# Half-size blocks for the rest of the routed rows, and a new order of the attention steps, in a decoder layer with eight experts

## The reference

```python
x = x + linear_attention(LN(x))          # q, k = elu(.) + 1; q (k^T v) / (q . sum k + eps), per batch
x = x + softmax(q k^T / 16) v            # q from LN(x), k and v from the context, with biases
xf = LN(x)                               # 4096 rows
shared = gelu(xf @ Wfc_s + bfc_s) @ Wproj_s + bproj_s        # 256 -> 1024 -> 256
gate = softmax over the two largest of xf @ Wr               # 8 experts, 2 per row
routed = sum_e gate[:, e] * (gelu(xf @ Wfc[e] + bfc[e]) @ Wproj[e] + bproj[e])
x = x + shared + routed
```

## Time and profile before

| | |
|---|---|
| median of 3 runs | 862.61 us (862.16 to 863.2) |
| profiled execution, whole time | 864.7 us |
| its span | 863.0 us |
| PE / DVE / ACT / POOL busy | 92% / 73% / 41% / 28% |
| attention steps | from the start to about 266 us |
| shared blocks, routed blocks | about 266 to 441 us, 441 to 852 us |

### The profile page before, as it was taken

The page is one execution under the profiler, slowest core; times in us unless marked ns, Lnnn a source line. Parts: engine busy times, 40 slices in busy tenths (PEclk is TensorE's granted clock), DMA queues, the critical chain, the costliest instruction groups (busy, mean ns, idle before and its releaser), DMA issues.

```text
span 863.0 us, 21653 instructions
## 1 busy us (share of the span) xinstructions
PE 797.6 (92%) x6791; PEld 671.2 (78%) x6791; DVE 632.9 (73%) x2006; ACT 356.8 (41%) x777; POOL 240.6 (28%) x221
## 2 busy tenths in 40 slices
PE   3889898899856999999999999999999999999994
PEld 1666676666644888888888888888888888888884
DVE  4578888988756998888876666666666666666663
ACT  4445454454323555555543333333333333333331
POOL 2210101101110025555503333333333333333333
PEclk9999999999956999999999999999999999999998
DMA  5465676765333567887743434355344434444430
GB/s 178 141 159 137 180 150 170 168 155 119 81 62 84 156 180 239 235 237 238 234 120 62 65 55 69 58 57 70 54 64 63 66 64 63 63 62 64 65 50 7
DMA packets 168045, 98.07 MB, mean 114 GB/s; under 512 B 110316, under 2 KB 163336, under 8 KB 167944
## 3 DMA queue, kind: packets, MB, share of 16 engines
q1 hardware_dynamic: 153640, 79.65, 38.3%
q0 software_dynamic: 14304, 17.10, 11.5%
HBM read 37.84 MB, written 37.88 MB: 88 GB/s over the span
## 4 chain that ended last, share of the span: by engine, by line
PE 67%; issue 22%; DVE 5%; DMA 2%; SPq 1%; ACT 1%; POOL 1%; POOLq 0%; DVEq 0%; ACTq 0%
PE bank_kv L1177 11%; PE bank_st L1163 11%; PE bank_kv L1179 11%; PE bank_st L1165 11%; PE bank_kv L1178 11%; PE bank_st L1164 11%; DMA stage_w<-in_L_ffn_Wfc_s 1%; POOL rstd L519 1%; DVE w_parts L961 1%; DVE w_parts L740 1%; PE bank_st L1097 1%; DVE expert_buffers L973 1%; DMA expert_buffers<-rows_by_expert 0%; SPq L345 0%; PE bank L1116 0%
## 5 line engine op out<-in xcount | busy, mean ns | idle before, releaser
L697 ACT ACTIVATE expert_buffers<-bank_st,bias_columns 128x256 f32<-128x256 f32 x440 | 207.0, 473 | 334.2 <-DVE expert_buffers L974 214.5
L1177 PE MATMUL bank_kv<-w_parts,expert_buffers 128*128 (+1 forms) x880 | 240.6, 273 | 1.0 <-DVE expert_buffers L974 1.0
L1178 PE MATMUL bank_kv<-w_parts,expert_buffers 128*128 (+1 forms) x880 | 240.4, 273 | 0.0
L1179 PE MATMUL bank_kv<-w_parts,expert_buffers 128*128 (+1 forms) x880 | 240.4, 273 | 0.0
L973 DVE TENSOR_SCALAR expert_buffers<-expert_buffers 128x256 f16<-128x256 f32 x440 | 130.2, 296 | 120.4 <-ACT expert_buffers L697 100.2
L974 DVE SCALAR_TENSOR_TENSOR expert_buffers<-expert_buffers 128x256 f16<-128x256 f32 x440 | 188.6, 429 | 15.1
L1163 PE MATMUL bank_st<-expert_buffers,w_parts 128*128 128x256 f16 x624 | 170.1, 273 | 1.3 <-DMA expert_buffers<-rows_by_expert 1.3
L1165 PE MATMUL bank_st<-expert_buffers,w_parts 128*128 128x256 f16 x624 | 170.1, 273 | 0.0
L1164 PE MATMUL bank_st<-expert_buffers,w_parts 128*128 128x256 f16 x624 | 170.1, 273 | 0.0
L563 POOL DMA_INDIRECT out<-expert_buffers,token x78 | 121.8, 1561 | 20.6 <-issue 20.2
L1177 PEld LDWEIGHTS bank_kv<-w_parts,expert_buffers 128*128 128x128 f16 x880 | 86.2, 98 | 15.1 <-DVE expert_buffers L974 2.9
(11 more groups left out here) (150 smaller groups left out, 1027.0 us busy)
## 6 DMA issues: line engine op xcount, KB each, us to landing
rows_by_expert<-w_parts SPq DMA_DIRECT2D x13, 795.0 KB, 5.5
stage_w<-in_L_ffn_Wfc SPq DMA_DIRECT2D x16, 512.0 KB
stage_w<-in_L_ffn_Wproj SPq DMA_DIRECT2D x16, 512.0 KB
expert_buffers<-in_L_ffn_bproj SPq DMA_DIRECT2D x39, 128.0 KB
rows<-in_x SPq DMA_DIRECT2D x16, 256.0 KB, 3.2
x_residual<-rows SPq DMA_DIRECT2D x16, 256.0 KB, 4.7
expert_buffers<-x_residual SPq DMA_DIRECT2D x16, 256.0 KB
out<-expert_buffers SPq DMA_DIRECT2D x16, 256.0 KB
```

Of the source, the lines that this page charges most:

```text
L697: act.activation(g32[f % 2], hid[f % 2][:, 0:BLK], ACT.Gelu_apprx_tanh, bias=bias, scale=UNSCALE).then_inc(s["gelu_done"], 1)
L1177: pe.matmul(y, g[:, 0, tile(t)], w_hi, start=f == 0 and t == 0, stop=False, skip_group_check=True)
L1178: pe.matmul(y, g[:, 0, tile(t)], w_lo, start=False, stop=False, skip_group_check=True)
L1179: op = pe.matmul(y, g[:, 1, tile(t)], w_hi, start=False, stop=f == FC - 1, skip_group_check=True)
```

## The change

Routed rows: each expert's rows fill blocks of 256 only as far as these get full, and the rest goes to blocks of 128. The kernel now has 25 full (`FULL`) and 21 half (`HALF`) routed blocks. In the half ones `up` moves 128 columns, ACT writes two chunks into one 256-column buffer, DVE splits them as a pair, `down` makes high-high and high-low in one matmul of 512 columns and low-high in one of 256, six chunks behind `up`, and the two halves of the result are added in `evacuate`. A half block has one scatter. The hidden layer has four PSUM banks for two. `route` has 20 parts in blocks 0 to 4 for 16 in 0 to 3; the scatters start at block 5 and are spread over 10 blocks (before: 4 and 11).

Attention steps: the first norm is applied by ACT (`norm_first`, from a small `shift` of DVE); the context products are made of three fp16 passes (DVE makes the low part of `ctxT`, and once those of `fold`, `wv` and the row vector); the largest two logits are found by `top_two`, for 15 batches in step 19 and for the last in step 20, with comparisons and reductions. The order on each engine is new. TensorE: state, scores, transposed context, attention, transposed probabilities, K and V, Q, probabilities times V, context products, logits. On SP the transposes of the first norm come after the store of x2. ACT converts the first weights behind the first norm's high part.

```diff
-    NRT = 2 * T // BLK + E - 1
+    FULL = (2 * T - E * (BLK - 1) + BLK - 1) // BLK
+    HALF = 2 * T // P + E - 1 - FULL * TB
...
-    SEND_FROM, SEND_BLOCKS = 4, 11
...
+    SEND_FROM, SEND_BLOCKS = 5, 10
...
+    def tiles_in(n):
+
+        return TB if n < FULL else 1
+
...
-        hid = [bank_st[:, c, :] for c in range(2)]
+        hid = [bank_st[:, 0, :], bank_st[:, 1, :], bank3[:, :], bank7[:, :]]
...
+        FIRST_HALF = NSH + FULL
+        LAG_FULL, LAG_HALF = 2, 6
...
-                if live(i + 1):
-                    turn_norm(0, i + 1)
...
                     sp.wait_ge(s["x2_stored"], b * 16)
                     sp.dma_start(tiles_of(x2_dram, b), rows[:, ds(b * TB, TB), 0:D])\
                         .then_inc(s["x2_stored"], 16)
+                if live(i + 1):
+                    turn_norm(0, i + 1)
+                b = i + 3
+                if 1 <= b < B:
+                    sp.wait_ge(s["x_loaded"], b * 16)
+                    sp.dma_start(rows[:, ds(b * TB, TB), 0:D], tiles_of(x_rows, b)).then_inc(s["x_loaded"], 16)
...
+            def load_xT(n):
+
+                if n >= 2:
                     sp.wait_ge(s["up_done"], FC * (n + (NSH - 1)))
-                sp.dma_start_transpose(xT[parity].rearrange("p l k n -> p (l k) n"),
-                                       rows16_dram[ds(n, 1)].rearrange("a r w -> (a r) w")).then_inc(s[f"xT_loaded{parity}"], 16)
+                dst = xT[n % 2] if n < FULL else xT_half[n % 2]
...
+            def norm_first(b):
+
+                act.wait_ge(s["shift_ready"], b)
+                got(act, "lo1_ready", b - 1)
+                for t in range(TB):
+                    op = act.activation(xn[0][:, t, :], rows[:, b * TB + t, 0:D], ACT.Identity,
+                                        bias=shift[:, t:t + 1], scale=rstd[:, t:t + 1])
+                op.then_inc(s["xn1_ready"], 1)
...
+                    got(act, "ctxT_done", i - 2)
+                    copy(ctxT16[:, :, 0, :], ctxT_ps, "ctxT_hi")
...
+                if live(i + 1) and i != -1:
+                    norm_first(i + 1)
+                if live(i - 3):
+                    got(act, "pT_done", i - 3)
+                    got_if(act, "pv_done", i - 4)
+                    copy(probT[0:CK, :], pT_ps[0:CK, :], "pT_copied")
+                if live(i + 1) and i != -1:
+                    high(0, i + 1)
...
+                    if G >= FIRST_HALF:
+                        pair = (c - FC * FIRST_HALF) // 2
+                        spare = g32[pair % 2]
+                        at = slice(f % 2 * P, f % 2 * P + P)
+                        if f % 2 == 0:
+                            act.wait_ge(s["g_ready"], FC * FIRST_HALF + pair - 1 if pair < 2 else c - 2)
...
+            def top_two(batches):
...
+                for j, out_hot in enumerate((best, second)):
+                    count_top(dve.tensor_tensor(part, values, of(j), ALU.is_equal))
+                    count_top(dve.tensor_tensor(part, part, below, ALU.mult))
+                    count_top(dve.tensor_reduce(at, part, AX.X, ALU.min))
+                    count_top(dve.tensor_tensor(out_hot, below, at_e, ALU.is_equal))
+                    if j == 0:
+                        count_top(dve.scalar_tensor_tensor(values, best, -3.0e38, values, ALU.mult, ALU.add))
+                        count_top(dve.tensor_reduce(top[:, 1, ts], values, AX.X, ALU.max))
...
+                sums_of = [(n, b) for n, b in ((0, i + 2), (1, i - 1), (2, i - 3)) if live(b)]
+                if live(i + 2) and i > 0:
+                    sums(i, 0, i + 2, len(sums_of) == 1)
...
+                    dve.scalar_tensor_tensor(shift[:, :], mv[:, 0, :, 0], -1.0, rstd[:, 0:TB], ALU.mult, ALU.mult)\
+                        .then_inc(s["shift_ready"], 1)
...
-                if live(i - 5):
-                    b = i - 5
-                    apart(dve)
-                    got(dve, "logits_copied", b)
-                    for t in range(TB):
-                        op = dve.max(max8[:, t, :], lg[:, t, :])
-                    chain(op, "max_step", b + 1, own=True)
-                    for t in range(TB):
-                        op = dve.max_index(max8_at[:, t, :], max8[:, t, :], lg[:, t, :])
-                    chain(op, "top_step", b + 1)
-                    dve.tensor_copy(top[:, ds(b * TB, TB), :], max8[:, :, 0:2])
-                    dve.tensor_copy(top_f[:, ds(b * TB, TB), :], max8_at[:, :, 0:2]).then_inc(s["top_ready"], 1)
...
+                if i in TOP_STEPS:
+                    top_two(TOP_STEPS[i])
...
+                    dve.tensor_tensor(ctxT16[:, :, 1, :], ctxT_ps, ctxT16[:, :, 0, :], ALU.subtract)\
+                        .then_inc(s["ctxT_lo"], 1)
...
+                elif part == 14:
+                    then(dve.tensor_tensor(beyond, place, over_t(full_rows), ALU.is_ge))
+                elif part == 15:
+                    then(dve.tensor_tensor(beyond, beyond, over_t(jump), ALU.mult))
+                    then(dve.tensor_tensor(place, place, beyond, ALU.add))
...
+                if G >= FIRST_HALF:
+                    y = ybuf[parity][:, 0, :]
+                    chain(dve.scalar_tensor_tensor(y, ysum[parity][:, 0, :], UNSCALE, b2blk, ALU.mult, ALU.add),
+                          "y_part", G - FIRST_HALF + 1)
+                    dve.scalar_tensor_tensor(y, ysum[parity][:, 1, :], UNSCALE, y, ALU.mult, ALU.add)\
+                        .then_inc(s["y_read"], 1)
+                    dve.wait_ge(s["y_read"], G + 1)
+                    dve.tensor_scalar(y, y, gate[parity][:, 0:1], None, ALU.mult).then_inc(s["y_ready"], 1)
...
+                    elif f % 2 == 1:
+                        pair = (c - FC * FIRST_HALF) // 2
+                        got(dve, "gelu_done", c)
+                        dve.wait_ge(s["down_done"], FC * FIRST_HALF + pair - 3 if pair < 4 else c - 7)
+                        g = gs[pair % 4]
+                        dve.tensor_scalar(g[:, 0, :], g32[pair % 2], A_SCALE, None, ALU.mult).then_inc(s["g_hi"], 2)
+                        dve.wait_ge(s["g_hi"], c + 1)
+                        dve.scalar_tensor_tensor(g[:, 1, :], g32[pair % 2], A_SCALE, g[:, 0, :], ALU.mult, ALU.subtract)\
+                            .then_inc(s["g_ready"], 2)
...
-                    got(pe, "ctxT_copied", b)
+                    got(pe, "ctxT_lo", b)
                     for m in range(DK):
                         for k in range(DK):
-                            pe.matmul(k2T_ps[:, m, :], fold[:, k, tile(m)], ctxT[:, k, :], start=k == 0, stop=k == DK - 1)
+                            for a, c in PASSES:
+                                pe.matmul(k2T_ps[:, m, :], fold16[:, k, a, tile(m)], ctxT16[:, k, c, :],
+                                          start=(k, a, c) == (0, 0, 0), stop=(k, a, c) == (DK - 1, 1, 0))
                     for k in range(DK):
-                        pe.matmul(row_ps[0:1, :], row_cols[:, k:k + 1], ctxT[:, k, :], start=k == 0, stop=k == DK - 1)
+                        for a, c in PASSES:
+                            pe.matmul(row_ps[0:1, :], row16_cols[:, k, a:a + 1], ctxT16[:, k, c, :],
+                                      start=(k, a, c) == (0, 0, 0), stop=(k, a, c) == (DK - 1, 1, 0))
                     for k in range(DK):
-                        op = pe.matmul(v2_ps[0:CK, :], ctxT[:, k, :], wv[:, k, :], start=k == 0, stop=k == DK - 1)
+                        for a, c in PASSES:
+                            op = pe.matmul(v2_ps[0:CK, :], ctxT16[:, k, a, :], wv16[:, k, c, :],
...
+                if G >= FIRST_HALF:
+                    g = gs[(c - FC * FIRST_HALF) // 2 % 4][:, :, f % 2 * P:f % 2 * P + P]
+                    y = bank_kv[:, parity, :].rearrange("p (l n) -> p l n", l=2)
+                    both = w2[:, ds(e * 4096 + ((f // 4) * 2048), 2048)].rearrange("p (l n) -> p l n", l=2)
+                    both = both[:, :, (f % 4) * 256:(f % 4) * 256 + D]
+                    pe.matmul(y, g[:, 0, :], both, start=f == 0, stop=False, skip_group_check=True)
+                    pe.matmul(y[:, 0, :], g[:, 1, :], both[:, 0, :], start=False, stop=f == FC - 1, skip_group_check=True)\
+                        .then_inc(s["down_done"], 1)
+                    return
...
                     if f == 2 and isinstance(G, int) and G == NSH:
                         pe.wait_ge(s["w2_lo"], HALVES)
                     up(G, parity, e, f)
-                    if f >= 2:
-                        down(G, parity, e, f - 2)
-                    elif before is not None:
-                        down(G - 1, 1 - parity, e_before, FC - 2 + f)
+                    d = FC * G + f - lag
+                    if d >= 0 and not (G == FIRST_HALF and f < LAG_HALF - LAG_FULL):
+                        down_lagging(d)
```

522 lines of the change are left out of this document (292 added, 230 removed).

## The result

The changed kernel takes 851.71 us (median of 7 runs, 848.70 to 856.37). The kernel before, run on the same chip, takes 862.61 us (7 runs, 859.75 to 865.96). The ratio is 0.9882, 95% interval 0.9847 to 0.9917. The change makes the kernel faster by 10.9 us, 1.2%: the interval excludes no change, but the gain stays under the 2% from which a version is called faster here. The forecast was 809, 54 us faster, in a range of 796 to 829: it was wrong. The profiled execution has a span of 853.1 us, against 863.0 before.

What follows compares the result with a forecast made beforehand. The prediction took TensorE to bound the expert blocks and DVE the attention steps, TensorE close behind. Its terms, the largest -29.1 and -16.6, summed to -54.2 us on a span of 863.0, giving 809 us, range 796 to 829.

Steps and rivals of the forecast that it cites:

- The new order, followed: Attention step: engine order traced through one step; every part is ready before it is wanted, step 11.9 us.
- the wait with least cover: Attention step on SP: the first norm's transpose, now behind the x2 store; landing at 6.4, wanted at 6.8 us.
- work terms (-16.6): Attention steps 4 to 13: less DVE and TensorE work cuts 13.56 to 11.9 us each, -16.6 us in all.
- Rival (C): Attention steps stay at 13.1 us because the first norm's transpose comes late behind the store: 824 us, chance 0.17.
- Half blocks: Routed blocks: 14 full blocks' worth goes, 21 half blocks of 5.6 us come; -29.1 us, from -22 to -35.
- Rival (B): Half blocks: 128-column matmuls go at 81 ns for 56, 25 us more in all: 834 us, chance 0.10.
- the chain through SP: Half blocks: meta copies, row load and transpose stall TensorE, 0.1 us a block, plus 0.2 for scatter packets.
- none binds by itself: Half blocks: ACT, DVE (4.9 us) and POOL (3.9 us) each keep up with TensorE's 5.3 us.
- Rival (D): Half blocks take 6.2 us through the meta, rows, transpose chain or scatter landing, 13 us more: 822 us, chance 0.12.
- the drain: Steps 16 to 20: DVE's max work goes, dearer context part and `top_two` overrun; -3.0 us, from +1 to -6.
- (E): Half blocks: stalls take TensorE's clock down, at 0.50 a block is 10.6 us, 105 more: 914 us, chance 0.03.
- The shared blocks: Shared blocks 1 to 4: 17 more DVE instructions for route parts cost +2.5 us, from 0 to +4.2.

Runs made afterwards that it cites:

- experiment 1: Changed kernel with SyncE issuing the load of batch i+3's x first in its attention step: 832.36 us, ratio 0.9592.
- experiment 2: Changed kernel with VectorE's sums of x moved behind those of x1, late in its step, SyncE's order as changed: 829.57 us, ratio 0.9576.
- experiment 3: Changed kernel with SyncE's x load directly ahead of the x2 store: 824.74 us in a single run.
- experiment 9: Two variants of experiment 7, single runs: no expert number read in half blocks, 806.54 us; fixed expert-0 addresses in full blocks too, 808.18 us.
- experiment 10: Experiment 6 with the 20 route parts three to a shared block over blocks 0 to 6: 821.39 us, ratio 0.9515.
- experiment 7: Experiment 6 with half blocks taking expert 0's weights from fixed addresses, without register steps; a measurement only: 804.84 us, ratio 0.9348.
- experiment 4: Changed kernel with four buffers for the half blocks' transposed rows, so transposes may start one block earlier: 849.09 us, ratio 0.9815.
- experiment 5: Changed kernel with TensorE reading the next block's expert number inside the running block: 858.99 us, ratio 0.9919.
- experiment 6: Changed kernel with SyncE's x load first in its step and four buffers for the half blocks' transposed rows: 821.62 us, ratio 0.9546.
- experiment 8: Experiment 6 with TensorE reading the next block's expert number inside the running block: 819.80 us, ratio 0.9528.

## Why the prediction was wrong

**Attention steps: the step that failed.** "The new order, followed ... All fit, with little room", and "SP's old order had the store last; now the first norm's transpose stands behind it ... the wait with least cover". I followed the store and the transposes but not SP's x load, which the same edit put behind both. And I had `sums(i, 0, i + 2)` only within DVE's total work, where its new place, first in DVE's step, puts the softmax, and through the probabilities K and V, behind a transfer. The runs show it at both ends (experiments 1 to 3). With the wait gone the ten steps are 11.70 us: the forecast of 11.9 was nearly right, and so was the sum of TensorE's work, which had 11.55. So the work terms (-16.6) were right for a kernel that had the x load in time. Rival (C) had the wrong transfer and only part of the loss: 13.1 us a step, where the seven steps at full clock took 13.72 and all ten 14.75 in the mean. That they are longer than before (13.56) is due to the three steps in which the clock fell; a fall of the clock in the attention steps stands in no term and no rival.

**Half blocks: a term too small.** The pace of 56 ns at 128 columns is confirmed: the up matmuls start 0.05 to 0.06 us apart, and eight column blocks of 0.66 us, with 48 of them and the down part, make 5.28 us (forecast 5.3). Rival (B) falls: no run shows its 81 ns, which it puts midway between 56 and 109; the runs show 55 to 56 ns. The 0.3 us that I added for the chain through SP has the right size: taking that wait away gives 6.2 us in 21 blocks, 0.30 a block. That is luck in part. I had every block lose a little, with a landing of 2.5 us; in truth eight blocks waited, for transposes that took up to 5.4 us, while the longer block gave them 0.7 us more room. The kernel before showed such landings in a row that I passed over, that of the routed rows themselves (median 3.2, up to 5.1 us):

```profile
expert_buffers<-rows_by_expert SPq DMA_TRANSPOSE x39, 3.2
```

Also, a block of 5.3 and a down part of 0.325 put TensorE's need at t + 5.6, not at t + 5.45; that slip is worth under 0.1 us a block. What the sum lacked was the instruction stream of TensorE itself: with fixed addresses 124.9 us become 109.8, 0.72 a block. I wrote that "none binds by itself" of ACT, DVE and POOL, and didn't ask it of TensorE's sequencer, whose register steps were there in the full blocks, six per column block of 1.31 us (in the kernel before 624 each at L1163 and L1165 and 312 each at L1177 and L1178, in 39 blocks), and cost nothing there (10.48 us with and without them, experiment 9). A column block of a half block has five in 0.66 us. 5.6 + 0.72 is 6.3 (6.25 measured). The forecast's range for the block ended at 6.2. Rival (D) had just this size, 6.2, but for the chain alone, which is under a third of the loss: its number is luck too.

The remaining 3.1 us of the routed part: I took 14 full blocks as 146.7 us, but the last one of before is shorter, since nothing follows it (38 spacings in 395.4 us, where 38 x 10.48 would be 398.2, which is 2.8 of it).

**Right as forecast:** the end (-2.5 for -2.3), the drain (-2.8 for -3.0), steps 14 and 15 (-1.7 for -1.6; they have no x to wait for, since there is no batch 16), the clock of 1.00 in half blocks, against (E). The start gave 3.0 us more than thought. The shared blocks cost 3.4 for 2.5. That the route parts are the cause wasn't shown: experiment 10 spaced them out and found nothing.

The measured 851.71 lies even above the 837 that the prediction had for (C) and (D) together: the rivals named both places, but (C) had the wrong transfer and less than half of the loss of the ten steps (12 us of 28.6), and (D) had one of the two causes.

**Why both together matter.** Without the wait for x, the wait for the transposed rows and the register steps the kernel is at 804.84 (experiment 7), 4 us below the forecast. The forecast was a sound sum of work. It missed one wait, the fall of the clock in three of the steps with this wait (0.50, where experiments 1 to 3 have 1.00), and one stream of instructions that has no row among the busy ones. What makes the address steps lie open at the start of a half block, and there alone, stays partly open: moving the number's read gave 0.06 us a block, taking all the address steps out gave 0.72, and which of them holds up the first matmuls wasn't separated.

**Open: the shared blocks.** From the last logits to the first routed matmul the changed kernel took 179.5 us, experiments 1, 2, 4 and 5 from 184.2 to 186.9, and all others 179.1 to 181.6, with the same code there (but for experiment 10). The four long ones are the four that were run in one series, on the same chip as experiments 6 to 8, so it may be a state of that series and not of their code. Between 300 and 410 us they have ACT waits that nothing in the profile explains, and the other runs of the changed code have none; here those of experiment 1:

```profile
ACT expert_buffers L746 <- issue: 6.3, 8, 1.0
ACT w_parts L726 <- issue: 1.2, 2, 1.0
```

TensorE idles eight times there, 4.0 us in all, seven of them for DVE's g parts (2.4 us in 4 in the changed kernel). The kernel before has such ACT waits too, 4.2 us in 6, but its TensorE idled only 0.5 us there. What starts this wasn't found. It is the 6 us that experiment 1 lacks against the sum of experiment 6, and it has no part in the account of the changed kernel, which doesn't show it.

## What to carry to other kernels

When an instruction is moved to the front of an in-order engine's step, look up what it waits for and where that now stands in the queue that issues it: a transfer moved later and its consumer moved earlier by the same edit cost 28 us here, though both engines had less work. When blocks are halved, halve the matmul time in the sum but not the sequencer's steps: here they went from six to five per column block, while its time went from 1.31 to 0.66 us, and address arithmetic that cost nothing under matmuls of 256 columns cost 0.72 us of 5.95, 12% of a block, at 128. And a new wait isn't bounded by the time before: in three of ten steps here the clock of the engine behind it fell as well.

## What the runs showed of the hardware

- Matmuls of 128 columns, each with its own weights, started 55 to 56 ns apart (experiment 7: 749.16, 749.22, 749.28, 749.33), where those of 256 columns started 109 ns apart (96 of them in a full block of 10.48 us).
- In the three steps of the changed kernel in which TensorE stood idle for 4.03, 2.68 and 3.98 us ahead of L1218, the granted clock fell to 0.50 (windows 92.80:94.80, 137.10:139.10 and 167.90:169.90), and 12 matmuls of 512 columns (L1227) took 4.31, 4.44 and 4.02 us instead of 2.75; with 1.4 to 2.0 us, in the seven other steps, it stayed at 1.00.
- Taking out TensorE's register steps, four of 46 ns and one of 32 per column block of 0.66 us (experiment 6, L1311, L1313 and L1327), gave back 0.72 us per half block (5.95 to 5.23, experiments 6 and 7), nearly all of it at the block's start, and nothing in a full block (10.48 us with six per column block and without them, experiment 9).
- A transpose of 128 rows took from 2.7 to 5.4 us from its issue to landing in the half blocks of the changed kernel (L501, 19 of them, median 3.5), where 2.5 had been taken from other transposes of the kernel before.
